# Joining two 64-lane halves of a scan result: on VectorE, from two buffers, in place of a TensorE product and a ScalarE copy

## The chip, the cores and the metric

The kernel runs on one core of one Trainium2 chip. The metric is the device time of one launch in microseconds (us), which handles all eight images. TensorE is called PE, VectorE DVE, ScalarE ACT, GpSimd POOL and SyncE SP, as in the profile.

## The reference, cut to what matters

The reference is a vision model of two layers on a tensor of 8 images, 96 channels, 64 x 64 positions. The part that this change touches is the end of the first layer's selective scan and the layer norm behind it:

```
# D_INNER = 192 channels, K = 4 directions, L = 64*64 positions
out_y = selective_scan(xs, dts, A, Bs, Cs, Ds, dt_b)       # (b, 4, 192, L)
inv_y = flip(out_y[:, 2:4], axis=-1)
wh_y, invwh_y = out_y[:, 1] and inv_y[:, 1] with H and W exchanged
y = out_y[:, 0] + inv_y[:, 0] + wh_y + invwh_y             # (b, 192, L)
y = layer_norm(y over the 192 channels, on_g, on_b)
y = y * silu(z)
attn = einsum('bhwd,cd->bhwc', y, out_proj_w)              # 192 -> 96
x1 = inp * skip_scale + attn                               # then LN2, 3x3 convolutions, channel
                                                           # attention, linear attention, FFN in fp8
```

## The kernel before

Images are processed one after another. Each image goes through `prep_a`, `prep_b` (projections and the depthwise convolution), `scan` and `post`. Each of these is a block: all engines start it together, after all of them have ended the one before. Within a block every engine has its own hand-written list of instructions and waits for the others by semaphores.

**The scan.** 192 channels are 128 + 64. The first 128 channels are scanned in four directions, with 128 lanes each. The remaining 64 channels of two directions share one pass of 128 lanes: lanes 0 to 63 hold the row-wise direction, lanes 64 to 127 the column-wise one. A pass is called T; there are six (T = 0 to 5), each of four chunks of 1024 positions. T = 5 is the last pass, with the 64-channel rest in both backward directions. Its result is in `py` (PSUM), and `take_y` on ACT copies it into `y5`: lanes 0 to 63 as they are (L1176), lanes 64 to 127 turned from columns to rows (L1178). So `y5` holds two halves that still have to be added.

**The post block.** It works on eight tiles j of 512 positions, named by `sl(j)`. `staggered` (in the helpers) writes a software pipeline: each stage has a lag, and in step t an engine runs each of its stages on tile t - lag, the stage with the largest lag first. The stages that matter here, with their lags:

- PE: `fold` (0), `var_192` (2), `out_proj` (4), `ln_sum` of x1 (5, a product with `ones_c`, L519), `ln_sum` of the squares (6, L519), `cab1` (9).
- ACT: `yr_copy` (0), `on_square` (0), `ln_root` (2, 6), `ln_square` (5), `ln2_affine` (7).
- DVE: `on_center` (0), `on_unit` and `gate` (3), `skip` (4), `ln_center` (5), `skip2` (6), `ln_unit` (7), `sides` (10).
- POOL: adds the squares of the 64 channels to those of the 128 (L1665), tile by tile.

The chain of one tile: `fold` multiplies `y5` with `fold_w` (two identity matrices under each other), which gives the sum of the two halves in PSUM (L1402), and gets the mean over 192 channels from two products with `ones_di`, of `ya` (L1405) and `y5` (L1406, all 128 lanes, so the halves need not be joined for it). ACT copies the sum to `yrc` (L1566). DVE subtracts the mean from `ya` (L1687) and `yrc` (L1689). ACT squares both (L1570, L1571), POOL adds them (L1665), PE makes the variance (L1413), ACT the reciprocal root (L534, L536), DVE multiplies (L1694, L1696) and gates (L1705, L1708), PE projects (L1419 with 128 rows, L1420 with 64 rows), and DVE adds the skip (L1713). `ln_center` (L524), `skip2` (L1719) and `ln_unit` (L541) are DVE's part of the next layer norm. SP loads the gates and `x_nat2` (L1377 to L1381) at the start of the block.

`wait_free(engine, freed, j, 2)` makes a stage wait until tile j - 2 has freed its bank. An fp32 product of 512 columns shows in the trace as two matmuls.

Of the kernel before, what the change touches and what calls it, by code (L numbers as in the profile page):

```python
# [29 lines left out]
DR = DI - DA  # L30
# [82 lines left out]
def build(nc, x, weights, phase_weights, setup_weights, out, gate_dram, gn_dram):  # L113
# [8 lines left out]
    def put(name, shape, dt):  # L122

        size = int(np.prod(shape[1:])) * (4 if dt == F32 else 2 if dt in (BF16, F16) else 1)
        t = nc.alloc_sbuf_tensor_at(name, shape, dt, offset=place[0])
        place[0] += (size + 31) // 32 * 32
        return t
# [6 lines left out]
    a_neg = put("a_neg", [128, 6, NS], F32)  # L134
    fold_w = put("fold_w", [128, 128], F32)
    d_sum = put("d_sum", [128, 2], F32)
# [18 lines left out]
    def big(name, slot, parts=128):  # L155
        return at(name, [parts, L], F32, slot)
# [56 lines left out]
    yr = big("yr", 5 * KB16)  # L213
    y5 = big("y5", 0)
    KB4 = SC * 4
# [55 lines left out]
    with ExitStack() as ctx:  # L271
# [9 lines left out]
        bt_mm bt_out dut_mm dut_out dbut_made turned""".split()  # L281
        post_names = """x_tok_in tok_parts tok_dve tok_mean_mm tok_var_mm tok_act back_first back_in yr_mm
        yr_copied on_mean_mm on_centered on_squared on_var_mm on_log on_rsqrt on_unit sq_added gated
        out_mm x1_ready ln2_mean_mm ln2_centered ln2_squared ln2_var_mm ln2_log ln2_rsqrt ln2_unit
# [106 lines left out]
        with nc.Block() as block:  # L391
# [22 lines left out]
            def _(dve):  # L414
# [8 lines left out]
                nc.vector.tensor_copy(conv_w[:, :], scol(setup, "conv_w"))  # L423
                low, up = col("ident")[:, 0:DR], col("ident")[:, DR:128]
                nc.vector.tensor_tensor(fold_w[:, 0:DR], low, up, ALU.add)
                nc.vector.tensor_tensor(fold_w[:, DR:128], low, up, ALU.add)

                for half in range(2):
# [59 lines left out]
        def sl(j):  # L488

            return slice(j * CH, (j + 1) * CH)  # L490
# [9 lines left out]
        def staggered(*stages):  # L500


            for t in range(NCH + max(lag for lag, _ in stages)):
                for lag, stage in sorted(stages, key=lambda s: -s[0]):
                    if 0 <= t - lag < NCH:
                        stage(t - lag)
# [424 lines left out]
        def scan():  # L931
# [65 lines left out]
            with nc.Block() as block:  # L997
# [167 lines left out]
                def _(act):  # L1165
# [3 lines left out]
                    def take_y(T, at, g):  # L1169

                        if g == 0:
                            act.wait_ge(S["parts_in"], 24 * 16)
                            act.wait_ge(S["bc_stored"], 12 * 16)
                        act.wait_ge(S["y_summed"], g + 1)
                        if T == 5:
                            act.copy(y5[0:DR, span(at * SC, SC)], py[0:DR, :])  # L1176
                            by_row = y5[DR:128, :].rearrange("p (h w) -> p h w", w=W)
                            last = act.copy(by_row[:, :, span(at * (SC // H), SC // H)],  # L1178
                                            py[DR:128, :].rearrange("p (w h) -> p h w", h=H))
                        else:  # L1180
                            last = act.copy(chunk(yr if T == 2 else ya, T, at), like(py[:, :], T))  # L1181
                        last.then_inc(S["y_taken"], 1)
# [183 lines left out]
        def post(img, b):  # L1366
            bank = dict(zip(("yr0", "on_mean0", "on_var", "out", "ln2_mean", "ln2_var", "yr1", "on_mean1"),
                            sum(ps, [])))
            bank.update(cab1_0=bank["yr0"], cab1_1=bank["yr1"], sum0=bank["on_mean0"], sum1=bank["on_mean1"])
            bank.update(cab2_0=bank["on_var"], cab2_1=bank["out"], ca1=bank["ln2_mean"], ca2=bank["ln2_var"])  # L1370
            bank.update(zip(("t1_mean", "t1_var", "kv0", "kv1", "kvt", "m", "f"), sum(ps, [])))
            bank.update(zip(("attn0", "t2_mean", "t2_var", "y", "h0", "h1", "h2", "attn1"), sum(ps, [])))
            with nc.Block() as block:
# [23 lines left out]
                def _(pe):  # L1397

                    def fold(j):

                        wait_free(pe, S["on_centered"], j, 2)
                        pe.matmul(bank[f"yr{j % 2}"], fold_w[:, :], y5[:, sl(j)], start=True, stop=True)\  # L1402
                          .then_inc(S["yr_mm"], 1)
                        mean = bank[f"on_mean{j % 2}"]
                        pe.matmul(mean, col("ones_di"), ya[:, sl(j)], start=True, stop=False)  # L1405
                        pe.matmul(mean, col("ones_di"), y5[:, sl(j)], start=False, stop=True)\  # L1406
                          .then_inc(S["on_mean_mm"], 1)
# [15 lines left out]
                    def cab1(j):  # L1423

                        if j == 0:
                            pe.wait_ge(S["back_in"], 64)
                            pe.wait_ge(S["cpad_zero"], 2)
                        if j < 2:
                            pe.wait_ge(S["yr_copied"], NCH - 1 + j)
                        pe.wait_ge(S["ln2_ready"], min(j + 2, NCH))  # L1430
                        wait_free(pe, S["sides_out"], j, 2)
                        for t in range(3):
                            mm = pe.matmul(bank[f"cab1_{j % 2}"][0:C, :], phase_col(post_w, "cab1", C)[:, t, :],  # L1433
                                           cpad[:, rows(j, t), :], start=(t == 0), stop=(t == 2))
                        mm.then_inc(S["cab1_mm"], 1)
# [58 lines left out]
                    def kv_sum(j):  # L1494
# [5 lines left out]
                        if j == NCH - 1:  # L1500
                            mm.then_inc(S["kvt_mm"], 1)

                    staggered((0, fold), (2, var_192), (4, out_proj),
                              (5, lambda j: ln_sum(pe, j, x1, S["x1_ready"], bank["ln2_mean"], S["ln2_centered"],
# [56 lines left out]
                def _(act):  # L1561
                    ln_exp_tables(act)

                    def yr_copy(j):
                        act.wait_ge(S["yr_mm"], j + 1)
                        act.copy(yrc[:, sl(j)], bank[f"yr{j % 2}"][0:DR, :]).then_inc(S["yr_copied"], 1)  # L1566

                    def on_square(j):
# [46 lines left out]
                    def kv_copy(j):  # L1615
                        for i in (2 * j, 2 * j + 1):
# [4 lines left out]

                    staggered((0, yr_copy), (0, on_square),
                              (2, lambda j: ln_root(act, j, bank["on_var"], S["on_var_mm"], rs, S["on_log"],
# [59 lines left out]
                @block.vector  # L1683
                def _(dve):
                    def on_center(j):
                        dve.wait_ge(S["on_mean_mm"], j + 1)
                        dve.tensor_tensor(ya[:, sl(j)], ya[:, sl(j)], bank[f"on_mean{j % 2}"], ALU.subtract)  # L1687
                        dve.wait_ge(S["yr_copied"], j + 1)
                        dve.tensor_tensor(yrc[:, sl(j)], yrc[:, sl(j)], bank[f"on_mean{j % 2}"][0:DR, :], ALU.subtract)\  # L1689
                           .then_inc(S["on_centered"], 1)  # L1690

                    def on_unit(j):
# [66 lines left out]
                    def weigh(j):  # L1759

                        if j == 0:
# [4 lines left out]
                                                 ALU.mult, ALU.add).then_inc(S["x2_ready"], 1)  # L1766

                    staggered((0, on_center), (3, on_unit), (3, gate), (4, skip),
                              (5, lambda j: ln_center(dve, j, x1, bank["ln2_mean"], S["ln2_mean_mm"], cen2,
# [193 lines left out]
```

## Time and profile before

| | us |
|---|---|
| median of 3 runs | 11820.38 |
| lowest, highest | 11805.1, 11823.1 |
| the profiled execution | 11786.2 |
| its span | 11784.4 |
| PE busy | 10415.9 (88%) |
| DVE busy | 10483.9 (89%) |
| ACT busy | 9335.6 (79%) |
| POOL busy | 9496.4 (81%) |

The span is the stretch that the profiler recorded; it is repeated eight times, once per image. In the first image the post block begins at 1316.7 us and ends at 1511.7 us. The other images have the same shape. Busy shares are averages over scan and post; they say little about a single stage, which is why the rows below are taken from the stretch in which the changed instructions stand.

### The profile page before, as it was taken

What the parts mean: (1) busy time and instruction counts of PE and PEld (TensorE: products, weight loads), DVE (VectorE), ACT (ScalarE), POOL (GpSimd) and SP (SyncE); (2) the same over time, 40 slices, a digit from 0 to 9 for tenths busy, and PEclk for the clock granted to TensorE, in tenths of its full rate; (3) what the DMA queues carried; (4) which work ended last, traced back from release to release, by engine and by line L of the source; (5) the groups of instructions that cost most, each with busy time, mean ns of one, the idle gap of its engine ahead of it and who ended that gap; (6) DMA issues with size and microseconds to landing.
All of it is one profiled execution on the core that took longest, in us unless ns stands there. A gap on an engine that the chain in (4) does not pass through costs nothing. (4 is left out here: it accounts for less than half of the span.)

```text
span 11784.4 us, 124896 instructions
## 1 busy us (share of the span) xinstructions
PE 10415.9 (88%) x35584; PEld 4882.5 (41%) x35584; DVE 10483.9 (89%) x7561; ACT 9335.6 (79%) x20418; POOL 9496.4 (81%) x4213
## 2 busy tenths in 40 slices
PE   7989889888898988989889898888988989889898
PEld 3444334443344433444334443344433444334443
DVE  7999789997899978999789997899978999789996
ACT  6888678886788867888678886788867888678886
POOL 5999469994699946999469994699946999469993
PEclk9999999999999999999999999899999999999999
DMA  5777547774477745777457774577745777457773
GB/s 148 224 223 224 121 144 224 224 222 114 149 223 225 223 109 154 224 224 221 105 157 224 223 223 103 159 223 224 222 101 162 222 225 224 98 166 222 227 221 88
DMA packets 673215, 2191.42 MB, mean 186 GB/s; under 512 B 160400, under 2 KB 162448, under 8 KB 661968
## 3 DMA queue, kind: packets, MB, share of 16 engines
q1 hardware_dynamic: 672528, 2183.44, 63.4%
q8 instruction: 287, 4.70, 0.2%
q14 instruction: 400, 3.28, 0.1%
HBM read 2085.75 MB, written 67.44 MB: 183 GB/s over the span
## 5 line engine op out<-in xcount | busy, mean ns | idle before, releaser
L1360 POOL TENSOR_TENSOR state<-state,c_sb 128x1024 f32<-128x1024 f32 x3072 | 7183.9, 2381 | 210.4 <-DMA c_sb<-bc 109.6
L1110 PE MATMUL ps<-state,wt 128*128 128x512 f32 x12288 | 5736.9, 600 | 64.5 <-ACT ya L1181 26.2
L1328 DVE TENSOR_TENSOR_SCAN state<-decay,carry,ps 128x1024 f32<-128x1024 f32 x1728 | 3987.8, 2337 | 41.3 <-issue 6.1
L1110 PEld LDWEIGHTS ps<-state,wt 128*128 128x128 f32 x12288 | 2263.3, 191 | 2253.2 <-issue 1933.2
L1234 ACT ACTIVATE dbu_t<-du_t,b_t 128x128 f32<-128x128 f32 (+1 forms) x10176 | 2951.0, 366 | 25.3 <-PE ps L1101 25.3
L1253 ACT ACTIVATE decay<-delta,a_neg 128x1024 f32<-128x1024 f32 x2304 | 2640.7, 1146 | 0.0
L1349 POOL TENSOR_TENSOR dbu<-b_sb,du 128x1024 f32<-128x1024 f32 x768 | 1822.9, 2374 | 180.1 <-DVE du L1333 157.3
L1315 DVE TENSOR_TENSOR ps<-ps,du 128x1024 f32<-128x1024 f32 x1288 | 1554.6, 1207 | 40.0 <-PE ps L1055 39.9
L1188 ACT COPY carry<-state 128x1 f32<-128x1 f32 x3072 | 568.2, 185 | 1250.9 <-DVE state L1328 1234.9
L1055 PE MATMUL ps<-parts,sel 114*128 114x512 bf16 (+1 forms) x2576 | 794.5, 391 | 791.2 <-DVE state L1328 790.1
L1328 DVE TENSOR_TENSOR_SCAN state<-ps,carry,dbu 128x1024 f32<-128x1024 f32 x576 | 1347.6, 2340 | 110.8 <-POOL dbu L1349 93.3
L1328 DVE TENSOR_TENSOR_SCAN state<-decay,ps 128x1024 f32<-128x1024 f32 x576 | 1296.3, 2277 | 14.3 <-PE ps L1101 2.8
L1101 PE MATMUL ps<-wt,dbu_t 128*128 128x128 f32 x8128 | 1093.7, 278 | 149.4 <-DVE state L1328 148.5
L1101 PEld LDWEIGHTS ps<-wt,dbu_t 128*128 128x128 f32 x8128 | 939.3, 142 | 639.2 <-issue 324.0
L1253 ACT ACTIVATE ps<-delta,a_neg 128x1024 f32<-128x1024 f32 x768 | 852.9, 1111 | 0.0
L1055 PEld LDWEIGHTS ps<-parts,sel 114*128 114x128 bf16 (+1 forms) x2576 | 170.8, 97 | 1626.1 <-DVE state L1328 1480.2
L1680 POOL CAST h<-h16b 128x1536 fp8e5<-128x1536 f16 x64 | 116.1, 1815 | 836.9 <-DVE h16b L1808 836.9
L304 ACT ACT_TABLE_LOAD x409 | 524.7, 1283 | 67.0 <-DMA x_tok<-x 20.2
L1328 DVE TENSOR_TENSOR_SCAN state<-ps,dbu 128x1024 f32<-128x1024 f32 x192 | 437.3, 2278 | 57.9 <-POOL dbu L1349 57.6
L1067 PE MATMUL ps<-parts,dt_w 114*128 114x512 bf16 (+1 forms) x1536 | 382.6, 393 | 29.9 <-PEq L696 29.9
L1665 POOL TENSOR_TENSOR sqa<-sqa,sqr 64x512 f32<-64x512 f32 x64 | 91.0, 1422 | 333.5 <-ACT sqr L1571 333.5
L768 PE MATMUL ps<-pad_a,conv_diag 128*128 128x512 f32 x640 | 276.6, 593 | 11.2 <-PEq L546 11.2
(227 smaller groups left out, 9633.2 us busy)
## 6 DMA issues: line engine op xcount, KB each, us to landing
c_sb<-bc SPq DMA_DIRECT2D x2048, 512.0 KB, 4.6
c_sb<-bc SPq DMA_DIRECT2D x2048, 256.0 KB, 5.9
b_sb<-bc SPq DMA_DIRECT2D x512, 512.0 KB, 3.9
b_sb<-bc SPq DMA_DIRECT2D x512, 256.0 KB, 4.0
gates<-gate_a SPq DMA_DIRECT2D x8, 2048.0 KB, 6.8
x_tok<-x SPq DMA_DIRECT2D x256, 48.0 KB, 1.8
gn<-gn_t SPq DMA_DIRECT2D x8, 1536.0 KB, 7.1
gate_a<-gates SPq DMA_DIRECT2D x8, 1536.0 KB, 10.6
```

The costliest lines, as they stand in the source:

```text
L304: act.add_instruction(mybir.InstLoadActFuncSet(name=nc.get_next_instruction_name(), act_func_set_id=which, ins=[], outs=[]))
L1055: mm = pe.matmul(bank[:, q * CH:(q + 1) * CH], sel[own, n, first:first + 128], part_cols(at, 2 * (T // 3), q, own), start=True, stop=True)
L1067: mm = pe.matmul(pc[:, q * CH:(q + 1) * CH], dt_w[own, p, w, :], part_cols(at, k, q, own), start=(i == 0 and p == 0), stop=(i == len(ways) ...
L1101: mm = pe.transpose(pb[n % 2][:, j * 128:(j + 1) * 128], src[:, j, :], col("ident"))
L1110: mm = pe.matmul(py[:, q * CH:(q + 1) * CH], col("ident"), state[:, slot(g, n), q * CH:(q + 1) * CH], start=(n == 0), stop=False)
L1188: act.copy(carry[:, n:n + 1], state[:, slot(g, n), last:last + 1]).then_inc(S["carried"], 1)
L1234: last = act.activation(dbu_t[turn % TRING][:, j, part], du_t[:, j, part], ACT.Copy, scale=b_t[:, g % 2, j, i:i + 1])
L1253: act.activation(pb[n % 2][:, :] if made(g, n) == BY_POOL else decay[:, n % 2, :], delta[:, g % 2, :], ACT.Exp, scale=a_neg[:, T, n:n + 1] ...
L1315: dve.tensor_tensor(pb[n % 2][:, :], pb[n % 2][:, :], du[:, g % 2, :], ALU.mult)\
L1328: dve.tensor_tensor_scan(state[:, slot(g, n), way], rate, what, 0.0 if fresh else carry[:, n:n + 1], ALU.mult, ALU.add)\
L1349: pool.tensor_tensor(dbu[:, :], b_sb[:, :], du[:, g % 2, :], ALU.mult)\
L1360: pool.tensor_tensor(state[:, slot(g, n), :], state[:, slot(g, n), :], c_sb[:, n % CRING, :], ALU.mult).then_inc(S["weighted"], 1)
```

## The change

The last pass no longer writes both halves into one buffer. Lanes 64 to 127 of `py` now go to lanes 0 to 63 of a second buffer, `y5c`, which lies where the first two directions' projections (`parts`) were, no longer read in that pass. Both halves then stand on the same lanes, and DVE adds them in a new function, `yr_sum`, straight into `yrc`. The first two tiles are added at the start of the block; tile j + 2 is added behind `on_center(j)`. PE's `fold` becomes `mean_192`: its product with `fold_w` is gone, and the second product of the mean reads `yrc`, of 64 rows, where it read `y5`, of 128; it waits for `yr_summed`. ACT's `yr_copy` is gone with the waits for it in `on_center` and `cab1`. The constant `fold_w` and the two DVE instructions that make it at the start of the program are gone.

```diff
-    y5 = big("y5", 0)
+    y5 = big("y5", 0, DR)
+    y5c = big("y5c", 2 * KB16, DR)
...
                             act.copy(y5[0:DR, span(at * SC, SC)], py[0:DR, :])
-                            by_row = y5[DR:128, :].rearrange("p (h w) -> p h w", w=W)
+                            by_row = y5c[:, :].rearrange("p (h w) -> p h w", w=W)
...
-                    def fold(j):
+                    def mean_192(j):
 
                         wait_free(pe, S["on_centered"], j, 2)
-                        pe.matmul(bank[f"yr{j % 2}"], fold_w[:, :], y5[:, sl(j)], start=True, stop=True)\
-                          .then_inc(S["yr_mm"], 1)
                         mean = bank[f"on_mean{j % 2}"]
                         pe.matmul(mean, col("ones_di"), ya[:, sl(j)], start=True, stop=False)
-                        pe.matmul(mean, col("ones_di"), y5[:, sl(j)], start=False, stop=True)\
+                        pe.wait_ge(S["yr_summed"], j + 1)
+                        pe.matmul(mean, col("ones_di", DR), yrc[:, sl(j)], start=False, stop=True)\
                           .then_inc(S["on_mean_mm"], 1)
...
-                        if j < 2:
-                            pe.wait_ge(S["yr_copied"], NCH - 1 + j)
...
-                    def yr_copy(j):
-                        act.wait_ge(S["yr_mm"], j + 1)
-                        act.copy(yrc[:, sl(j)], bank[f"yr{j % 2}"][0:DR, :]).then_inc(S["yr_copied"], 1)
...
-                    staggered((0, yr_copy), (0, on_square),
+                    staggered((0, on_square),
...
+                    def yr_sum(j):
+                        dve.tensor_tensor(yrc[:, sl(j)], y5[:, sl(j)], y5c[:, sl(j)], ALU.add).then_inc(S["yr_summed"], 1)
+
                     def on_center(j):
                         dve.wait_ge(S["on_mean_mm"], j + 1)
                         dve.tensor_tensor(ya[:, sl(j)], ya[:, sl(j)], bank[f"on_mean{j % 2}"], ALU.subtract)
-                        dve.wait_ge(S["yr_copied"], j + 1)
                         dve.tensor_tensor(yrc[:, sl(j)], yrc[:, sl(j)], bank[f"on_mean{j % 2}"][0:DR, :], ALU.subtract)\
                            .then_inc(S["on_centered"], 1)
+                        if j + 2 < NCH:
+                            yr_sum(j + 2)
...
+                    yr_sum(0)
+                    yr_sum(1)
                     staggered((0, on_center), (3, on_unit), (3, gate), (4, skip),
```

DVE's order in the post block, from the centring of tile 2 (`ya`, then `yrc`) to the gating of tile 0, before:

```order
L1687 TENSOR_TENSOR ya<-ya,ps 128x512
L1689 TENSOR_TENSOR yrc<-yrc,ps 64x512
L1694 SCALAR_TENSOR_TENSOR ya<-ya,wt,rs 128x512
L1696 SCALAR_TENSOR_TENSOR yrc<-yrc,wt,rs 64x512
L1705 SCALAR_TENSOR_TENSOR ya<-ya,wt,gate_a_122 128x512
L1708 SCALAR_TENSOR_TENSOR yrc<-yrc,wt,gate_r_123 64x512
```

The same place now (line numbers are those of the changed kernel; `y_106` is `y5`):

```order
L1679 TENSOR_TENSOR ya<-ya,ps 128x512
L1680 TENSOR_TENSOR yrc<-yrc,ps 64x512
L1675 TENSOR_TENSOR yrc<-y_106,y5c 64x512
L1687 SCALAR_TENSOR_TENSOR ya<-ya,wt,rs 128x512
L1689 SCALAR_TENSOR_TENSOR yrc<-yrc,wt,rs 64x512
L1698 SCALAR_TENSOR_TENSOR ya<-ya,wt,gate_a_122 128x512
L1701 SCALAR_TENSOR_TENSOR yrc<-yrc,wt,gate_r_123 64x512
```

One addition, that of tile 4, stands between the centring and the next step's first instruction.

PE's order from the variance of tile 1 to the first output projection, before (`y_107` is `y5`):

```order
L1413 MATMUL ps<-sqa,wt 128x512
L1402 MATMUL ps<-y_107,fold_w 128x512
L1405 MATMUL ps<-ya,wt 128x512
L1406 MATMUL ps<-y_107,wt 128x512
L1419 MATMUL ps<-ya,wt 96x512
L1420 MATMUL ps<-yrc,wt 96x512
```

The same place now:

```order
L1408 MATMUL ps<-sqa,wt 128x512
L1399 MATMUL ps<-ya,wt 128x512
L1401 MATMUL ps<-yrc,wt 128x512
L1414 MATMUL ps<-ya,wt 96x512
L1415 MATMUL ps<-yrc,wt 96x512
```

One product of three is gone, and the last of the mean reads `yrc` where it read `y5`.

## Rows read from the trace of the kernel before

**Rows 1.** Windows of post: span, each engine's busy us, PEclk, DMA share, GB/s
```profile
1316.70:1334.20 17.50, 14.57 (x32) 5.62 (x32) 8.69 (x12) 10.07 (x17) 4.38 (x3) 1.00 0.96 248
1334.20:1363.50 29.30, 29.28 (x65) 10.68 (x65) 27.04 (x39) 18.41 (x33) 7.26 (x7) 1.00 0.33 78
7182.70:7188.00 5.30, 5.26 (x9) 2.27 (x10) 0.71 (x2) 1.86 (x2) 0.00 (x0) 0.68 0.80 192
```

**Rows 2.** PE's timeline, one step: start, duration, engine, line, operands, count
```profile
1348.08 1.13 PE L1413 MATMUL ps<-sqa,wt 128*128 128x512 f32 x2
1349.04 1.02 PE L1402 MATMUL ps<-y,fold_w 128*128 128x512 f32 x2
1349.90 1.02 PE L1405 MATMUL ps<-ya,wt 128*128 128x512 f32 x2
...
1353.34 1.02 PE L1419 MATMUL ps<-ya,wt 128*96 128x512 f32 x2
1354.29 1.10 PE L1420 MATMUL ps<-yrc,wt 64*96 64x512 f32 x2
1355.31 1.13 PE L1413 MATMUL ps<-sqa,wt 128*128 128x512 f32 x2
...
1363.51 2.74 PE L1433 MATMUL ps<-cpad,post_w 96*96 96x512 f32 x6
```

**Rows 3.** DVE's timeline, same step, later skip; in brackets idle before and releaser
```profile
1353.02 0.68 DVE L541 TENSOR_TENSOR cen<-cen,rs 96x512 f32<-96x512 f32 x1
1353.62 0.74 DVE L1719 SCALAR_TENSOR_TENSOR x<-x,wt,x_nat 96x512 f32<-96x512 f32 x1
1354.29 0.67 DVE L524 TENSOR_TENSOR cen<-x,ps 96x512 f32<-96x512 f32 x1
1355.42 0.74 DVE L1713 SCALAR_TENSOR_TENSOR x<-gn,wt,ps 96x512 f32<-96x512 f32 x1 [0.46 <-PE ps L1420]
...
1359.05 0.69 DVE L1687 TENSOR_TENSOR ya<-ya,ps 128x512 f32<-128x512 f32 x1 [0.24 <-PE ps L1406]
...
1369.89 0.74 DVE L1713 SCALAR_TENSOR_TENSOR x<-gn,wt,ps 96x512 f32<-96x512 f32 x1 [1.20 <-PE ps L1420]
```

**Rows 4.** PE's timeline, first steps of post, image 1
```profile
1316.72 1.10 PE L1402 MATMUL ps<-y,fold_w 128*128 128x512 f32 x2 [2.37 <-PEq L997]
...
1323.42 1.12 PE L1413 MATMUL ps<-sqa,wt 128*128 128x512 f32 x2 [1.32 <-POOL sqa L1665]
```

**Rows 5.** DVE's timeline, first steps of post, image 1
```profile
1319.57 0.69 DVE L1687 TENSOR_TENSOR ya<-ya,ps 128x512 f32<-128x512 f32 x1 [15.81 <-PE ps L1406]
...
1327.16 0.69 DVE L1687 TENSOR_TENSOR ya<-ya,ps 128x512 f32<-128x512 f32 x1 [3.74 <-PE ps L1406]
...
1328.36 0.74 DVE L1694 SCALAR_TENSOR_TENSOR ya<-ya,wt,rs 128x512 f32<-128x512 f32 x1
...
1329.69 0.73 DVE L1705 SCALAR_TENSOR_TENSOR ya<-ya,wt,gate_a 128x512 f32<-128x512 f32 x1
1330.35 1.75 DVE L1708 SCALAR_TENSOR_TENSOR yrc<-yrc,wt,gate_r 64x512 f32<-64x512 f32 x1
```

**Rows 6.** POOL's timeline, additions of squares of tiles 2 and 6
```profile
1329.70 1.85 POOL L1665 TENSOR_TENSOR sqa<-sqa,sqr 64x512 f32<-64x512 f32 x1 [3.76 <-ACT sqr L1571]
...
1354.36 1.27 POOL L1665 TENSOR_TENSOR sqa<-sqa,sqr 64x512 f32<-64x512 f32 x1 [5.27 <-ACT sqr L1571]
```

**Rows 7.** ACT's group of the turned copy: busy us, mean ns, idle before
```profile
L1178 ACT COPY y<-ps 64x1024 f32<-64x1024 f32 x32 | 32.2, 1007 | 0.4
```

**Rows 8.** SP's timeline: issue of the reload of x
```profile
1320.31 0.43 SPq L1381 DMA_DIRECT2D x_nat<-x  x1
```

**Rows 9.** DMA issues of post in image 1: us from issue to landing
```profile
x_nat<-x SPq DMA_DIRECT2D x1, 1536.0 KB, 25.1
```

**Rows 10.** PE's timeline at the start of the fifth image's post
```profile
7182.74 1.31 PE L1402 MATMUL ps<-y,fold_w 128*128 128x512 f32 x2 [2.37 <-PEq L997]
...
7187.09 1.02 PE L1402 MATMUL ps<-y,fold_w 128*128 128x512 f32 x2
```

More of the change, by code:

```diff
@@ L134, in build @@
     a_neg = put("a_neg", [128, 6, NS], F32)
-    fold_w = put("fold_w", [128, 128], F32)
     d_sum = put("d_sum", [128, 2], F32)
@@ L281, in build @@
         bt_mm bt_out dut_mm dut_out dbut_made turned""".split()
-        post_names = """x_tok_in tok_parts tok_dve tok_mean_mm tok_var_mm tok_act back_first back_in yr_mm
-        yr_copied on_mean_mm on_centered on_squared on_var_mm on_log on_rsqrt on_unit sq_added gated
+        post_names = """x_tok_in tok_parts tok_dve tok_mean_mm tok_var_mm tok_act back_first back_in
+        yr_summed on_mean_mm on_centered on_squared on_var_mm on_log on_rsqrt on_unit sq_added gated
         out_mm x1_ready ln2_mean_mm ln2_centered ln2_squared ln2_var_mm ln2_log ln2_rsqrt ln2_unit
@@ L423, in _ @@
                 nc.vector.tensor_copy(conv_w[:, :], scol(setup, "conv_w"))
-                low, up = col("ident")[:, 0:DR], col("ident")[:, DR:128]
-                nc.vector.tensor_tensor(fold_w[:, 0:DR], low, up, ALU.add)
-                nc.vector.tensor_tensor(fold_w[:, DR:128], low, up, ALU.add)
                 for half in range(2):
@@ L1366, in post @@
         def post(img, b):
-            bank = dict(zip(("yr0", "on_mean0", "on_var", "out", "ln2_mean", "ln2_var", "yr1", "on_mean1"),
+            bank = dict(zip(("side0", "on_mean0", "on_var", "out", "ln2_mean", "ln2_var", "side1", "on_mean1"),
                             sum(ps, [])))
-            bank.update(cab1_0=bank["yr0"], cab1_1=bank["yr1"], sum0=bank["on_mean0"], sum1=bank["on_mean1"])
+            bank.update(cab1_0=bank["side0"], cab1_1=bank["side1"], sum0=bank["on_mean0"], sum1=bank["on_mean1"])
             bank.update(cab2_0=bank["on_var"], cab2_1=bank["out"], ca1=bank["ln2_mean"], ca2=bank["ln2_var"])
@@ L1501, in kv_sum @@
                             mm.then_inc(S["kvt_mm"], 1)
-                    staggered((0, fold), (2, var_192), (4, out_proj),
+                    staggered((0, mean_192), (2, var_192), (4, out_proj),
                               (5, lambda j: ln_sum(pe, j, x1, S["x1_ready"], bank["ln2_mean"], S["ln2_centered"],
```

## The prediction

> **What bounds the kernel now.** I read the page for the busy shares first, and they settle nothing: PE and DVE are both near 89% over scan and post together. The change adds and removes work only in the first part of post (scan keeps its two copies per chunk), so I went to the windows of that part, then to the timelines of PE, DVE and POOL there. The windows show three different states [rows 1]. In the first 17.5 us PE works 14.6 and DVE 8.7: the pipeline is filling, and latency decides. From 1334.2 to 1363.5 PE is busy in 29.28 of 29.30 us, DVE in 27.04. So the bound there is PE, with DVE close behind it. The reader should see the same in one step: PE goes from one variance product to the next in 7.23 us (1348.08 to 1355.31) without a gap [rows 2], and in that step DVE waits twice for PE, 0.46 us for the projection and 0.24 us for the mean [rows 3]. ACT and POOL are never late here except as links in the filling. Behind the last fold DVE still waits for PE (1.20 us before the skip at 1369.89 [rows 3]); that skip starts a stretch in which DVE works through, so I take its start as the mark at which a gain is handed on to the rest of the image.
>
> **The change, part by part.**
>
> PE, removed: one product per tile, 64 in all. From its start to the next product's is 0.86 us (1349.04 to 1349.90) [rows 2]; eight tiles make 6.9 us per image.
>
> PE, altered: the mean's second product has 64 rows instead of 128. The trace has such a product in L1420: behind the 128-row L1419 it starts after 0.95 us, and the next one starts 1.02 us later, where equal shapes take 0.86; the product behind the variance then starts 0.96 us after it [rows 2]. I charge 0.09 + 0.16 + 0.10 = 0.35 us per tile. The bounds are 0 (if the extra is not due to the rows) and 0.35. The net saving of PE is then 0.5 us per tile, 4.1 per image, 6.9 without the extra. The Trainium skill, "TensorEngine Tiling (Array Packing)", Key Properties, says that a change of tiling mode drains TensorE. By it the added change between 128 and 64 rows costs in every tile, as the rows say; without it the sum below would be about 0.6 us per image better.
>
> DVE, added: eight additions of 64x512 from two SBUF buffers. L541 is such an instruction on 96 lanes: 0.68 us, and the next starts 0.60 behind it [rows 3]. I take 0.60. A step of DVE is now: L541 0.60, L1719 0.67, L524 0.60, L1713 0.67, four of L1694 to L1708 at 0.66, two centrings at 0.60, in all 6.4 us. With an addition it is 7.0 us, against PE's 7.23 before and 6.7 now. So DVE becomes the bound of every step that has an addition, steps 0 to 5. Steps 6 and 7 have none and run at DVE's 6.4.
>
> ACT, removed: the copies. ACT has 18.4 us of work in the 29.3 [rows 1] and waits for the centring in each step, so nothing comes of it. POOL's work is unchanged.
>
> The new wait: the mean's second product waits for an addition made two steps before; only for tiles 0 and 1 is it fresh. Both additions can be done while PE makes the first product, 1316.7 to 1317.7, so I charge nothing. Were they late, what is queued behind is all of PE's step, and DVE waits for that; the price would be up to 0.3 us per image.
>
> The turned copy writes lanes 0 to 63 instead of 64 to 127, same count, 1.007 us each, 32 times [rows 7]. No row shows a difference by lanes; bounds -0.1 to +0.1 us a copy, of which only the last of an image is on the path: below 1 us in sum. The setup loses two small DVE instructions, under 1 us.
>
> Now the schedule of image 1 by hand. First centring: 2.85 us behind the first product (1316.72 to 1319.57) [rows 4, 5]; less 0.86, plus 0.17 for entering 64 rows and the longer end (1.10 against 1.02): 0.69 earlier. The tile's chain (centre, squares, POOL's addition, variance) starts that much earlier, so the variance product stands at 1322.7 instead of 1323.42 [rows 4]; the mean of tile 2 behind it again saves 0.69, and the centring of tile 2 starts at 1325.8 instead of 1327.16 [rows 5]. Then DVE's addition comes between it and L1694, which starts at 1327.6 instead of 1328.36: 0.76 earlier. In steps 3 to 6 DVE pays 0.6 per addition but no longer waits for PE (the waits it had were of this size), so the lead stays near 0.8: centring of tile 6 at 1351.0 instead of 1351.8. Step 7 has no addition and no wait: 6.4 instead of 7.2, the centring of tile 7 at 1357.4 instead of 1359.05 [rows 3]. The first `cab1` waits for that centring's squares and the affine behind it on ACT, 1360.65 instead of 1363.51 [rows 2]. Behind it PE makes two sums and the projection of tile 5, and the skip starts at 1367.05 instead of 1369.89 [rows 3]. That is 2.8 us.
>
> One thing checked there: `skip2` of tile 0 needs the reload of x, issued at 1320.31 and landed 25.1 us later, at 1345.4 [rows 8, 9]; it now starts about 1346.4. One us more of gain would meet that load.
>
> POOL's additions of squares matter to DVE. Where one starts while L1705 runs, it takes 1.85 instead of 1.27 us, and L1708 takes 1.75 instead of about 0.73 [rows 5, 6]. Three DVE instructions per image lose 1.0 us in this way before. In my schedule POOL's addition starts 1.27 us behind the end of a centring, so with an addition of 0.6 in between it falls on L1694 to L1713 in steps 3 to 5, as before, and just behind `skip2` in steps 6 and 7. I count three losses before and three now.
>
> Sum: 8 x 2.8 = 22.7 us. In some images the first products run slower: in the fifth the first fold takes 1.31, the second starts 4.35 us after it instead of about 2.65, and the granted clock there is 0.68 on average, so part of it at 1.2 GHz [rows 1, 10]. There the removed product was worth more, about 0.6 us more in each of the four images with such a start; against it stands that PE now has longer gaps. I let them cancel and take 23 us. The profiled execution of 11786.2 becomes 11763. It lay 34 us (0.3%) below the median of 11820.4; set against the median, the forecast is 11797 us, 0.19% less.
>
> **The rivals.**
>
> A, PE's saving comes through whole. For it: PE was the bound of steps 5 to 9. Against it: DVE had only 0.7 us of waiting per step, and it now gets 0.6 of work. It needs the 64-row product to cost nothing extra and the additions to fall into waits. Time: 6.9 x 8 = 55 us less, 11765; with the first condition alone 3.4 to 4 x 8 = about 30 less, 11790.
>
> B, DVE takes it back. The Trainium skill, "SBUF — State Buffer", gives DVE and GpSimd one shared port pair, an exclusive lock held for a whole instruction, for a DVE instruction with two SBUF inputs; rows 5 and 6 agree, with 1.75 and 1.85 us. In terms of rows: each POOL addition that now starts inside `yr_sum` or `skip2` costs DVE 1.0 us. Against it: `yr_sum` ends 0.6 us behind the centring and POOL starts at 1.27. Two such meetings per image (steps 6 and 7, where `skip2` ends within 0.1 us of POOL's start) take 2.0 of the 2.8: 6 us less, 11814, no change that can be told.
>
> C, slower: PE's clock. PE works denser before than now; in the filling it had a gap of 1.32 us [rows 4] and one like it, now some four gaps of 1.5 to 2.4 us per image. In the fifth image, after a gap of 2.37 us (and a thin end of the scan), the clock was at its low level in the first products and cost 1.7 us. Should each of four gaps bring that, 6.8 - 2.8 = 4 us per image is lost: 32 us more, 11852. It decides from two extra falls per image on. Against it: in image 1 the same gap of 2.37 us and the one of 1.32 left the clock at 1.00 [rows 1, 4].
>
> **How the numbers follow.** The forecast has 0.52, A 0.15, B 0.22, C 0.11. What this kernel's measurement can tell from no change is about 0.2%, 24 us. The forecast's own range is 14 to 31 us less, so about half of it is beyond 24: 0.26; with 0.14 of A that is 0.40 faster. Of C, 0.08 is slower by more than 0.2%. The rest, 0.52, is within 0.2%. The range runs from 11772 (most of A kept, B and forecast in full) to 11820 (B in full, C out); the three runs alone span 18 us.
>
> **What would show it.** PE's step from variance to variance near 7.0 us instead of 7.23 while additions run and 6.4 after them, with gaps ahead of L1414 for DVE; no wait of DVE for PE at the skip or the mean in steps 5 to 8; the new group of 64 DVE instructions at 0.68 us, not 1.7; the first centring 2.2 us behind PE's first product; the first `cab1` at about 43.9 us behind it instead of 46.8. The prediction is wrong if DVE instructions of 1.75 us become more than three per image, if PE's matmuls of over 1 us multiply, or if the time saved by the first `cab1` is missing at the image's end, which would mean that something behind it did not depend on it.

## The result and the profile after

The change makes the kernel slightly slower: 11829.2 us (median of 22 runs, 11808.5 to 11843.7) against 11806.2 us for the kernel before (22 runs, 11798.2 to 11823.1). The ratio is 1.0016, with a 95% interval from 1.001 to 1.0022: 19 us more, where 23 us less were forecast. That is less than the 0.2% that the prediction took for the least that can be told, and yet the interval is clear of 1. Against the run-by-run scatter the profiled execution shown before the prediction (11786.2 us) was a low one, 20 us below this median; the changed kernel's profiled execution took 11823.4 us. The three runs of before that the prediction set out from had a median of 11820.4, 14 us above that of the 22; set against 11806.2, the forecast is 11783 us.

The changed kernel's page, span and busy shares:

```profile
span 11821.6 us, 124614 instructions
PE 10451.3 (88%) x35456; PEld 4867.6 (41%) x35456; DVE 10508.0 (89%) x7623; ACT 9303.4 (79%) x20354; POOL 9494.2 (80%) x4213
```

The shares say as little as they did before. The windows of post do: two of image 1, as in [rows 1], then the first 17.5 us of post in images 2 and 3 (same columns: span, busy us of PE, PE's weight loads, DVE, ACT and POOL, granted clock, DMA share, GB/s):

```profile
1316.30:1333.80 17.50, 17.50 (x19) 5.08 (x20) 8.74 (x14) 7.18 (x11) 3.70 (x3) 0.52 0.96 254
1333.80:1363.00 29.20, 27.60 (x57) 8.27 (x56) 28.78 (x41) 14.42 (x24) 8.21 (x7) 1.00 0.31 74
...
2786.60:2804.10 17.50, 15.04 (x20) 4.15 (x20) 10.38 (x15) 7.16 (x11) 4.96 (x3) 0.71 0.97 251
...
4260.70:4278.20 17.50, 15.09 (x20) 4.42 (x20) 10.36 (x15) 7.24 (x11) 4.96 (x3) 0.71 0.96 246
```

PE's granted clock is 0.52 in the first 17.5 us of image 1, where it was 1.00; 0.71 in images 2 and 3. An instruction at its low level (1.2 GHz) takes about twice as long, and so PE is busy for all 17.50 us with 19 matmuls (two make a product), where it had 32 before in 14.57. The trace of before has four products with `fold_w` in this window; they are 8 of the 13 missing matmuls, and the other five are work that PE had not reached. In image 1 the clock is full behind that. DVE is then busy in 28.78 of 29.20 us; 3.7 of them are five instructions that take 1.11 to 1.77 us instead of 0.74 while POOL adds squares. In images 2 and 3 the clock falls a second time, behind PE's wait for the first projection:

```profile
4278.48 1.67 PE L1414 MATMUL ps<-ya,wt 128*96 128x512 f32 x2 [2.66 <-DVE yrc L1701]
```

In image 1 the low stretch lasts 17.1 us; in image 3 there are two, of 10.2 and 6.8 us. Every image of the changed kernel has 14 to 17 us at the low clock in its fill, while before had none in four images and 3 to 7 us in the other four.

This is not one odd execution. The mean clock of a whole execution is 0.967 to 0.971 in all 22 runs of the changed kernel, and 0.972 to 0.976 in all 58 runs of the kernel before that were timed beside the experiments, on two chips.

The timeline of PE shows the same by instruction, in image 1, for the start of post, the first variance product, and two variance products later (start, duration, engine, line, operands, count; in brackets idle before and releaser):

```profile
1316.27 2.05 PE L1399 MATMUL ps<-ya,wt 128*128 128x512 f32 x2 [2.37 <-PEq L993]
1318.24 2.07 PE L1401 MATMUL ps<-yrc,wt 64*128 64x512 f32 x2
...
1324.25 2.07 PE L1408 MATMUL ps<-sqa,wt 128*128 128x512 f32 x2
...
1351.10 1.12 PE L1408 MATMUL ps<-sqa,wt 128*128 128x512 f32 x2
...
1357.84 1.12 PE L1408 MATMUL ps<-sqa,wt 128*128 128x512 f32 x2
...
1365.59 2.79 PE L1426 MATMUL ps<-cpad,post_w 96*96 96x512 f32 x6
```

DVE, same stretch, same columns:

```profile
1320.36 0.69 DVE L1679 TENSOR_TENSOR ya<-ya,ps 128x512 f32<-128x512 f32 x1 [2.80 <-PE ps L1401]
...
1330.08 0.69 DVE L1679 TENSOR_TENSOR ya<-ya,ps 128x512 f32<-128x512 f32 x1 [3.83 <-PE ps L1401]
...
1372.02 0.74 DVE L1706 SCALAR_TENSOR_TENSOR x<-gn,wt,ps 96x512 f32<-96x512 f32 x1 [1.05 <-PE ps L1415]
```

A product of 128 rows takes 2.05 us where it took 1.10 [rows 4], so the first centring comes 4.09 us behind PE's first product (1316.27 to 1320.36) instead of 2.85 [rows 4, 5]. The centring of tile 2 is 13.8 us behind it (10.4 before), the first `cab1` 49.3 (46.8), the mark of the prediction, the skip of tile 5, 55.75 (53.2). What is lost is lost by the centring of tile 2; from there to the mark the changed kernel is even a little quicker. Its step from variance to variance is 6.74 us against 7.23 [rows 2].

Image 5, where before had a slow start too [rows 10], shows what the schedule does when the clock happens to be high. PE first, then DVE:

```profile
7198.65 1.10 PE L1399 MATMUL ps<-ya,wt 128*128 128x512 f32 x2 [2.37 <-PEq L993]
7199.68 1.12 PE L1401 MATMUL ps<-yrc,wt 64*128 64x512 f32 x2
7200.73 2.07 PE L1399 MATMUL ps<-ya,wt 128*128 128x512 f32 x2
```

```profile
7200.84 0.69 DVE L1679 TENSOR_TENSOR ya<-ya,ps 128x512 f32<-128x512 f32 x1 [0.90 <-PE ps L1401]
```

The first centring is 2.19 us behind the first product, as forecast (2.2). But the very next product takes 2.07: here the clock falls a moment later.

Last, the groups of instructions of the changed kernel that answer to DVE's side (busy us, mean ns of one, idle time before):

```profile
L1675 DVE TENSOR_TENSOR yrc<-y,y5c 64x512 f32<-64x512 f32 x64 | 42.8, 678 | 103.7 <-PEq L993 103.7
...
L1687 DVE SCALAR_TENSOR_TENSOR ya<-ya,wt,rs 128x512 f32<-128x512 f32 x64 | 50.8, 793 | 0.0
...
L1701 DVE SCALAR_TENSOR_TENSOR yrc<-yrc,wt,gate_r 64x512 f32<-64x512 f32 x64 | 55.3, 864 | 0.0
```

And the one of before that answers to L1687:

```profile
L1694 DVE SCALAR_TENSOR_TENSOR ya<-ya,wt,rs 128x512 f32<-128x512 f32 x64 | 62.6, 979 | 0.0
```

The additions take 0.68 us each, as L541 led to expect [rows 3]. DVE's meetings with POOL have not become more on the whole: the mean of L1687 fell by 186 ns. But this hangs on the clock. Up to the mark, the instructions that take over 0.15 us more than usual are three in each image of before; in the changed kernel they are six in image 1 and one in each other image, and with the clock held (e5 below) seven in each.

### The profile page after: what moved, and what is told of

Its sections match the earlier page's. It is cut to its first block and busy times, and to the rows that moved or that the text cites. A ratio compares the mean times of both kernels' runs of the same rounds, so it can differ in the third digit from the quotient of the medians.

```text
span 11821.6 us, 124614 instructions
## 1 busy us (share of the span) xinstructions
PE 10451.3 (88%) x35456; PEld 4867.6 (41%) x35456; DVE 10508.0 (89%) x7623; ACT 9303.4 (79%) x20354; POOL 9494.2 (80%) x4213
```

## The experiments

Two numbers are read for each kernel beside its time. The **mark** is the start of the skip of tile 5 behind PE's first product of post, mean over the eight images: 54.15 us before, 56.15 after. The **low-clock time** is taken from the granted clock in slices of 1 us: (1 - clock) x 2 us per slice, so that a slice at the low level counts as 1, summed over the first 47 us of the eight posts. It is 17 us before and 133 after (136 in some expectations, a coarser count of the same). All kernels but the three marked "one run" were timed in rounds beside the kernel before; ratios carry their 95% interval.

| kernel | ratio | mark, us | low-clock time, us |
|---|---|---|---|
| before | 1 | 54.15 | 17 |
| after | 1.0016 (1.001 to 1.0022) | 56.15 | 133 |
| e1_rows128 | 0.9992 (0.9983 to 1.0) | 52.52 | 71 |
| e2_before64 | 1.0015 (1.0007 to 1.0023) | 55.45 | 14 |
| e3_twice | 1.0003 (0.9995 to 1.0011) | 54.48 | 85 |
| e4_dummy | 1.0029 (1.0019 to 1.0039) | 57.95 | 48 |
| e5_fill64 | 0.9985 (0.9976 to 0.9994) | 51.39 | 0 |
| e6_fill128 | 0.9982 (0.9973 to 0.9991) | 50.66 | 0 |
| e7_fillbefore | 1.0002 (0.9993 to 1.0011) | 53.65 | 0 |
| e8_postfill | one run | 53.72 | 54 |
| e9_scanfill | one run | 54.48 | 71 |
| e10_onesrows | one run | 52.21 | 58 |

Mark and low-clock time come from one profiled execution of each kernel. Eight times the difference in the mark gives each ratio to within about 8 us: after +16 us (measured 19), e1 -13 (-9), e2 +10 (18), e3 +3 (4), e4 +30 (34), e5 -22 (-18), e6 -28 (-21), e7 -4 (+2). So most of what the change does is decided in the first 55 us of post.

### e1_rows128: the changed kernel, with 128 rows in the mean's second product

```diff
-    yrc = big("yrc", 5 * KB16, DR)
+    yrc = big("yrc", 5 * KB16)
...
-    pe.matmul(mean, col("ones_di", DR), yrc[:, sl(j)], start=False, stop=True)
+    pe.wait_ge(S["yrc_zero"], j + 1)
+    pe.matmul(mean, col("ones_di"), yrc[:, sl(j)], start=False, stop=True)
...
+    for j in range(NCH):
+        pool.memset(yrc[DR:128, sl(j)], 0.0).then_inc(S["yrc_zero"], 1)
```

> The changed kernel, but the mean's second product has 128 rows again: yrc is 128 lanes wide, POOL sets lanes 64 to 127 to zero tile by tile, and the product uses the full ones_di. Number of products as in the changed kernel. Theory R (a product of 64 rows is what keeps TensorE's clock at its low level in the first 12 to 17 us of post): the granted clock of the first 17.5 us of post is above 0.9 in most images (0.52 in image 1 of the changed kernel), the skip of tile 5 starts about 50 us behind PE's first product (56.2 us on average in the changed kernel, 54.2 before), and the time is about 11780 us, ratio to before 0.998. Theory D (one product less per tile makes PE's work too thin): the clock stays low, skip at 55.5 us or later, ratio 1.001.

Measured: 11797.8 us, ratio 0.9992 (0.9983 to 1.0), against 1.0016 for the changed kernel. The mark is 3.6 us earlier per image than in the changed kernel. The first 17.5 us of post in images 1 and 2:

```profile
1321.10:1338.60 17.50, 13.09 (x23) 4.91 (x24) 12.35 (x18) 8.33 (x13) 8.67 (x11) 0.82 0.96 246
...
2789.10:2806.60 17.50, 12.81 (x24) 4.73 (x25) 12.56 (x18) 8.07 (x13) 8.68 (x11) 0.90 0.96 245
```

The clock is 0.82 and 0.90 where it was 0.52 and 0.71; it is 0.82 to 0.90 in seven of the eight images. So the result lies between the two theories, the clock as well as the mark: both parts of the change have a share in the low clock. And PE's step, from variance to variance, in a steady stretch of image 4:

```profile
5753.35 1.13 PE L1409 MATMUL ps<-sqa,wt 128*128 128x512 f32 x2
...
5759.73 1.12 PE L1409 MATMUL ps<-sqa,wt 128*128 128x512 f32 x2
```

6.38 us. That is the step of before less the product removed (7.23 - 0.86 = 6.37 [rows 2]), and also the 6.4 forecast for DVE: here the two engines are level. With 64 rows the step is 6.74, 0.36 more, which is the 0.35 charged. So at full clock the 64 rows cost what was forecast; with two products in a step they also go with more time at the low clock, 133 us against 71.

### e2_before64: the kernel before, with a 64-row product in the mean

The upper half's share of the mean is left out here.

```diff
-    pe.matmul(mean, col("ones_di"), y5[:, sl(j)], start=False, stop=True)
+    pe.matmul(mean, col("ones_di", DR), y5[0:DR, sl(j)], start=False, stop=True)
```

> The kernel before with only one thing altered: the mean's second product reads lanes 0 to 63 of y5 alone (the upper half's share of the mean is left out). Three products per tile as before, no DVE addition, ACT's copy kept. Theory R: the clock stays low in the first 10 to 17 us of post, skip of tile 5 at 58 us or more behind the first product, 3 to 5 us per image lost: 11830 to 11845 us, ratio 1.002 to 1.0035. Theory D: the clock is as before, and the time is before's plus the 0.35 us that a 64-row product costs PE per tile, 2.8 us per image at most: 11806 to 11828, with post's first 17 us at the clock of before.

Measured: ratio 1.0015 (1.0007 to 1.0023). The windows of images 1 and 2, and one step of PE:

```profile
1315.00:1332.50 17.50, 15.32 (x32) 5.13 (x32) 8.69 (x12) 9.57 (x16) 4.37 (x3) 1.00 0.95 250
...
2788.40:2805.90 17.50, 15.37 (x29) 5.14 (x29) 7.62 (x11) 9.04 (x15) 4.38 (x3) 0.90 0.94 249
```

```profile
1347.26 1.13 PE L1413 MATMUL ps<-sqa,wt 128*128 128x512 f32 x2
...
1349.08 1.02 PE L1405 MATMUL ps<-ya,wt 128*128 128x512 f32 x2
1350.04 1.12 PE L1406 MATMUL ps<-y,wt 64*128 64x512 f32 x2
1351.09 1.10 PE L519 MATMUL ps<-sq,wt 96*96 96x512 f32 x2
...
1354.86 1.13 PE L1413 MATMUL ps<-sqa,wt 128*128 128x512 f32 x2
```

The step is 7.60 us instead of 7.23 [rows 2]: 0.37 us for the 64 rows, by themselves. But the clock in the fill is as before (14 us low against 17). So a 64-row product alone, with three products in a step, does not bring the clock down, and the theory that it does falls here. PE's time in the steps moves the mark by 1.3 us an image, 10 of the 18 us of slowdown; what the rest is, is not shown. The Trainium skill, "TensorEngine Tiling (Array Packing)", Key Properties, says that a change of tiling mode drains the engine. The 0.37 us would fit that; whether a 64-row product between others is such a change, no run here shows.

### e3_twice: e1 with each addition done twice

```diff
+    dve.tensor_tensor(rs[0:DR, sl(j)], y5[:, sl(j)], y5c[:, sl(j)], ALU.add)
     dve.tensor_tensor(yrc[0:DR, sl(j)], y5[:, sl(j)], y5c[:, sl(j)], ALU.add).then_inc(S["yr_summed"], 1)
```

> The version with 128 rows, with every addition of the halves made twice on DVE (the second result goes to rs, where it is overwritten). Prices the addition. If DVE is the bound of steps 0 to 5 as predicted, each of the four to six additions there costs its full 0.60 us: 2.4 to 3.6 us per image, 19 to 29 us over the run against the version with 128 rows. If the additions fall into waits for PE, nothing: within 5 us of it.

Measured: ratio 1.0003 (0.9995 to 1.0011), 0.0011 above e1; mark 2.0 us later per image. Eight additions of 0.60 are 4.8 us, so at most four tenths of the added DVE time reach the mark, and the rest falls into waits. At most, since the low-clock time rose as well, from 71 to 85 us. The 13 us lie between the two forecasts (5 and 19 to 29). The additions are not free, and they are not the loss either: e1, which has them all, is quicker than the changed kernel.

### e4_dummy: the changed kernel, with an unused product in the fold's place

```diff
+    pe.matmul(bank[f"side{j % 2}"], col("ident"), ya[:, sl(j)], start=True, stop=True)
     pe.matmul(mean, col("ones_di"), ya[:, sl(j)], start=True, stop=False)
```

> The changed kernel with a 128-row product put back in the removed one's place (identity by ya, result unused); the mean's second product keeps its 64 rows. Three products per tile as before. Theory D: the clock is back to what it was before, time near 11806, ratio 1.000. Theory R: the clock stays low as in the changed kernel, and each product costs time besides: 11835 to 11850 us, ratio 1.0025 to 1.004.

Measured: ratio 1.0029 (1.0019 to 1.0039), the slowest of all. Images 1 and 2, and PE's step:

```profile
1320.30:1337.80 17.50, 16.97 (x28) 5.29 (x28) 9.41 (x15) 7.19 (x11) 4.37 (x3) 0.80 0.96 253
...
2793.50:2811.00 17.50, 14.74 (x30) 5.04 (x30) 11.68 (x17) 7.25 (x11) 4.98 (x3) 0.96 0.97 235
```

```profile
1355.39 1.13 PE L1409 MATMUL ps<-sqa,wt 128*128 128x512 f32 x2
...
1362.99 1.12 PE L1409 MATMUL ps<-sqa,wt 128*128 128x512 f32 x2
```

Neither theory's forecast holds whole: the clock goes the way of the one, the time lies where the other put it. The clock recovers in part (133 us low become 48), but the product stands in every one of the eight steps, on PE's path: 7.60 us a step instead of 6.74. A higher clock is no gain when it is bought with products in the steps that PE bounds. The filler has to stand where PE waits. That led to the next three, made as a 2 x 2: clock held or not, change made or not.

### e5_fill64, e6_fill128, e7_fillbefore: unused products in PE's waits

The same filler in the changed kernel (e5), in e1 (e6) and in the kernel before (e7, there into the bank `ln2_var`): two unused products behind the scan's last sum, and 0, 1, 1, 2 behind the means of tiles 0 to 3.

```diff
+    pe.wait_ge(S["dut_out"], 6 * NSC)
+    for i in range(2): pe.matmul(pc[:, 0:CH], col("ident"), wt[:, 0:CH], start=True, stop=True)
...
+    for i in range((0, 1, 1, 2)[j] if j < 4 else 0):
+        pe.matmul(bank["side1"], col("ident"), wt[:, 0:CH], start=True, stop=True)
```

> The changed kernel, with products whose result is not used put into PE's waits: two behind the last sum of the scan (PE waits 2.37 us for the block's end there), none, one, one and two behind the means of tiles 0, 1, 2 and 3. Theory C (what the change lost is TensorE's clock, since PE has thinner work in the filling of the pipeline): low-clock time in the first 47 us of the eight posts falls from 136 us to below 50, the skip of tile 5 starts 51 to 53 us behind PE's first product (56.2 without), and the time falls below the kernel before, ratio 0.998 to 0.9995. Rival L (the loss is latency: the additions and the new wait on DVE's path, the clock only follows): mark at 56 or later, ratio 1.0016 or more, since PE gets more work.

> The same unused products in the version with 128 rows in the mean's second product. Theory C: low-clock time in the first 47 us below 30 us over the eight posts (71 without), mark near 50 us (52.5 without; 50.3 was worked out for a clock at its high level), ratio to before 0.997 to 0.998, about 11780. Rival L: mark and time as without them, ratio 0.999.

> The kernel before with the same unused products, the control. Its low-clock time in the first 47 us is only 17 us over eight posts, so theory C gives it at most about 1 us per image: ratio 0.999 to 1.0; where the products outlast a wait of PE it gets slower, up to 1.001.

Measured: 0.9985 (0.9976 to 0.9994), 0.9982 (0.9973 to 0.9991; expected was 0.997 to 0.998) and, for the control, 1.0002 (0.9993 to 1.0011). e5, images 1 and 2:

```profile
1321.70:1339.20 17.50, 16.78 (x34) 5.41 (x35) 13.37 (x19) 8.34 (x13) 5.38 (x4) 1.00 0.97 245
...
2793.30:2810.80 17.50, 16.77 (x34) 5.43 (x35) 13.37 (x19) 8.37 (x13) 5.37 (x4) 1.00 0.96 252
```

PE's timeline of e5: the filler of the scan, the first products of post, a filler (L1407), the first variance; then DVE's first centring:

```profile
1319.14 1.88 PE L1161 MATMUL ps<-wt 128*128 128x512 f32 x4
...
1321.68 1.10 PE L1402 MATMUL ps<-ya,wt 128*128 128x512 f32 x2 [0.66 <-PEq L993]
1322.71 1.12 PE L1404 MATMUL ps<-yrc,wt 64*128 64x512 f32 x2
...
1325.87 1.13 PE L1407 MATMUL ps<-wt 128*128 128x512 f32 x2
1327.72 1.13 PE L1413 MATMUL ps<-sqa,wt 128*128 128x512 f32 x2 [0.72 <-POOL sqa L1659]
```

```profile
1323.87 0.69 DVE L1684 TENSOR_TENSOR ya<-ya,ps 128x512 f32<-128x512 f32 x1 [0.90 <-PE ps L1404]
```

The clock is 1.00, the first product of post takes 1.10 us, the first centring is 2.19 us behind it, and DVE gets through 19 instructions in the window where the changed kernel had 14. Rival L had forecast a mark of 56 or later and falls. The 2 x 2 is read off the table. Without fillers the change moves the mark by +2.0 us; with the clock held (e7 to e5) by -2.26, where -2.8 was forecast, and the ratio by -0.0017 (1.0002 to 0.9985), 20 us of gain where 23 were forecast (30 us by the two medians, 11822.9 and 11792.5). The fillers do next to nothing for the kernel before (-0.5 us of mark, ratio 1.0002), so they are no gain of their own: they give back what the change takes away. From e6 to e5 the mark moves by 0.73 us: that is the 64-row product's price with the clock out of the way; in the ratio the intervals hide it. e6, with a first window of

```profile
1322.30:1339.80 17.50, 15.70 (x35) 6.27 (x36) 13.98 (x20) 8.37 (x13) 9.50 (x12) 1.00 0.97 245
```

has the lowest ratio of all kernels and is below the kernel before by 0.18%; e5 is not told apart from it.

With the clock held something else shows: the meetings of DVE and POOL. First `on_unit`'s instruction in e5 and the same one in e7, then one step of PE in e6:

```profile
L1692 DVE SCALAR_TENSOR_TENSOR ya<-ya,wt,rs 128x512 f32<-128x512 f32 x64 | 70.7, 1104 | 0.0
L1699 DVE SCALAR_TENSOR_TENSOR ya<-ya,wt,rs 128x512 f32<-128x512 f32 x64 | 49.0, 766 | 0.0
```

```profile
1351.93 1.13 PE L1414 MATMUL ps<-sqa,wt 128*128 128x512 f32 x2
...
1358.57 1.13 PE L1414 MATMUL ps<-sqa,wt 128*128 128x512 f32 x2
```

The change costs DVE 21.7 us over the run in this instruction alone, 2.7 us per image. In e5 most of it is hidden, since PE's step stays 6.74. In e6 the step is 6.64 us, where e1 had 6.38; DVE works through it without a gap, and one instruction of 1.01 instead of 0.74 us is the difference.

### e8_postfill, e9_scanfill: one half of the filler each

e8 is e5 without the two products at the scan's end, e9 is e5 without those behind the means.

> The changed kernel with the unused products in post alone (none, one, one and two behind the means of tiles 0 to 3), none behind the scan. Tells which wait of PE lets the clock fall. If the low clock is kept low by the thin work after it has fallen, these products bring it back soon: low-clock time in the first 47 us between 20 and 60 us over the eight posts, mark at 52 to 53 us. If the wait at the scan's end is all, near the changed kernel's 136 us and mark 56.

> The changed kernel with two unused products behind the last sum of the scan alone, none in post. If the wait at the scan's end is what starts the fall, low-clock time in the first 47 us is below 40 us and the mark at 51 to 53 us; if post's own waits start falls too, 60 to 110 us and mark at 53.5 to 55.5.

Measured: neither is enough (54 and 71 us at the low clock, against 0 with both). e8 has both cases in one execution, images 1 and 4:

```profile
1315.60:1333.10 17.50, 17.47 (x26) 5.53 (x27) 9.44 (x15) 7.24 (x11) 4.37 (x3) 0.71 0.96 250
...
5727.70:5745.20 17.50, 16.75 (x34) 5.43 (x35) 13.34 (x19) 8.39 (x13) 5.34 (x4) 1.00 0.95 246
```

DVE's skips of tile 5 in the two images; PE's first products stand at 1315.63 and 5727.73:

```profile
1370.65 0.75 DVE L1708 SCALAR_TENSOR_TENSOR x<-gn,wt,ps 96x512 f32<-96x512 f32 x1 [1.06 <-PE ps L1417]
...
5778.80 0.74 DVE L1708 SCALAR_TENSOR_TENSOR x<-gn,wt,ps 96x512 f32<-96x512 f32 x1 [1.06 <-PE ps L1417]
```

The same instructions, in the same order, in one execution: 55.0 us to the mark with the clock at 0.71, 51.1 with it at 1.00. This is the cleanest price of the clock, 3.9 us for 10 us at the low level, since nothing in the program differs and DVE's stretched instructions are alike in the two images. The expectation for e8 was met in the low-clock time (20 to 60 us) and missed in the mark (52 to 53); that for e9, with falls that start in post too, was met in both. The single times, 11826.1 us for e8 and 11831.9 for e9 beside 11804.4 for the kernel before, have the same sign.

### e10_onesrows: e1 with ones in the upper lanes and zero weights for them

```diff
-    pool.memset(yrc[DR:128, sl(j)], 0.0)
+    pool.memset(yrc[DR:128, sl(j)], 1.0)
-    pe.matmul(mean, col("ones_di"), yrc[:, sl(j)], start=False, stop=True)
+    pe.matmul(mean, ones_lo, yrc[:, sl(j)], start=False, stop=True)
```

> The version with 128 rows, but the added lanes 64 to 127 hold ones and meet weights of zero, instead of zeros that meet weights. Same instructions on PE. If the clock goes by what is issued and not by the values, low-clock time (71 us) and mark (52.5) stay within 15 us and 0.7 us of that version's; if the values matter, they move beyond that.

Measured: 58 us at the low clock and a mark of 52.21, against 71 and 52.52 with zeros; one run of 11796.6 us beside 11804.4. The values that are streamed in the added rows do not matter here, to within the 15 us and 0.7 us set before. The added products are zero in both kernels, so whether nonzero ones would act otherwise is not shown.

## Why the prediction was wrong

**The step that failed** is the last one of the sum: "There the removed product was worth more [...]; against it stands that PE now has longer gaps. I let them cancel and take 23 us." They do not cancel. Over the eight images the low-clock time in the fill goes from 17 to 133 us, 14.5 us more per image, and costs the forecast's whole gain and 16 to 19 us beside it: the mark is 4.8 us later than with the clock held (56.15 against 51.39), 38 us over eight images, where the term was put at nothing.

**Rival C was what happened**, at a chance of 0.11. It named rightly that the clock falls in the fill for want of PE's work. It priced four short falls, 6.8 us per image; the runs show one fall or two that last longer (17.1 us in image 1, 10.2 and 6.8 in image 3), at 4.8 us. The four gaps that it counted are not there in image 1: at the low clock PE's products fill them. What spoke against it in the prediction was a poor witness: that in image 1 of the kernel before two gaps left the clock at 1.00 [rows 1, 4] shows that the clock held under three products a step. It says nothing on two. The four images of before with a slow start (the fifth in [rows 10]) were the better witness: there the clock already fell in the first products, and the change takes work away exactly there. With them in view, 0.11 was too little.

**The clock.** The falls come in the fill, and products put into PE's waits remove them (133 us to 0). The Trainium skill, "TensorE: Matmul & The Clock Gate", section "HAM oscillation — how this bites in real kernels", says that long enough waits between groups of products let the clock fall back, again at each group. The trace agrees in kind. It shows besides that the clock stays low while PE is busy in 17.50 of 17.50 us, and that with two products in a step 64 rows in place of 128 go with more of it (71 to 133 us); why, no run shows.

**PE, removed and altered.** Right. The 64-row product was charged 0.35 us per tile and costs 0.37 (e2, where PE alone is the bound) and 0.36 (after against e1). PE's step was put at 6.7 us and is 6.74.

**DVE, added.** The size was right (0.68 us each, 0.60 from start to start in the forecast). "So DVE becomes the bound of every step that has an addition", with a step of 7.0 us, did not come true: a step of 6.74 us is PE's. The sum of 7.0 put the addition into the same step as `ln_unit` (lag 7) and `skip2` (lag 6); the last addition is made in step 5, before either of them runs. In e1 the step from 5753.35 has an addition and is 6.38 us, which a DVE step of 7.0 would not allow. That error was on the safe side and small.

**The schedule by hand.** Right wherever the clock is high: first centring 2.19 us behind the first product (forecast 2.2), mark at 51.1 in six of eight images of e5 (forecast 1367.05 - 1316.72 = 50.3, before 53.2). The gain per image with the clock held is 2.26 us, 0.5 less than the forecast 2.8; what took the half is not shown.

**The new wait** for `yr_summed` is not what ended any idle time of PE's matmuls in the lines above; charging nothing fits them. **Rival B**, that POOL's additions of squares hold DVE up: not in the changed kernel as it ran, where L1701 has 864 ns against 862 before and L1687 793 against 979. It is no cause of the loss. With the clock held it comes true in part: seven stretched instructions per image in e5, where the prediction counted three. Three of them are long (1.66 to 1.76 us), as it counted; it missed the shorter ones. **Rival A** is excluded: even with 128 rows and the clock held (e6) the gain is 0.18%, not 0.47%.

**What stays open.** Between 47 and 160 us of post the instructions are the same, yet the low-clock time there differs: 17 us before, 43 after, 55 in e5, 59 in e2, 48 in the control e7. With one profiled execution each, and the control above the changed kernel, this is not put down to the change. Why the fall comes in the first products of some images and a product later in others (image 5 of after) is open too. That e1 is faster than the kernel before rests on an interval that ends at 1.0.

## What to carry to other kernels

Taking a product from PE in a stretch where PE waits anyway can cost more than it saves: read the granted clock there, image by image, and where it already dips in some of them, give a further fall a large chance and a price of its own. Read "busy" on PE together with the clock, since a PE at its low level looks fully busy. Unused products put into PE's waits, never into the steps that PE bounds, tell whether the clock is the cause, and the same filler in the kernel before is the control that such a run needs. Once the clock is held, look again at the other engines: here DVE's meetings with POOL went from two or three an image to seven.

## What the runs showed of the hardware

- The clock's low level can cover a pipeline's whole filling: 0.52 over 17.5 us in image 1 of the changed kernel, in which PE was never idle by the busy count. A product of 128 rows and 512 columns takes 2.05 us then, 1.10 at the full clock.
- The fall is deepest where both parts of the change come together. Low-clock time over the eight images: three products of which the last has 128 rows, 17 us; three with 64 rows, 14; two with 128, 71; two with 64, 133 (one execution each).
- Whether added rows stream zeros or ones (with zero weights) makes little difference to it: 71 and 58 us.
- A 64-row fp32 product of 512 columns between 128-row ones costs 0.36 to 0.37 us more than a 128-row one, though it has half the rows.
- An instruction of `on_unit` or `gate` on DVE that meets POOL's addition of squares takes up to 1.76 us instead of 0.74, and POOL's addition up to 2.46 instead of 1.26 (e5, image 1).
